# Graph network and transformer kernel: the opening in a new order, the attributes' parts made by GpSimd, and the edge steps spread anew

## The reference

```
xn = layernorm(x)
# graph part
m = concat(xn[src], attr); t = relu(m @ gW1.T + gb1)      # 100000 x 256
h = concat(xn, segment_sum(t, dst)); y = relu(h @ gW2.T); y = y / max(|y|, 1e-12)
# mix part, 4 layers on xn
h = layernorm(x)*g+b;  x += linear_attention(h)  # softmax of k over nodes, of q over features
h = layernorm(x)*g+b;  x += gelu(h @ W1 + b1) @ W2 + b2    # 256 -> 1024 -> 256
# then
x = x + y + mix;  x = x + moe(layernorm(x))      # 16 experts, top 2, layernorm behind it
```

## Time and profile before

| | |
|---|---|
| median of 3 runs | 2307.67 us (2304.2 to 2311.34) |
| the profiled execution | 2316.51 us |
| its span, first to last instruction | 2314.7 us |
| busy: PE, DVE, POOL, ACT | 1936.4, 1443.2, 1357.0, 942.0 us |
| mean granted clock of TensorE | 0.933 |
| keys of layer 0 begin | 175.7 us |
| feed-forward of layer 0 begins | 303.6 us |

### The profile page before, as it was taken

How to read it: one execution, slowest core, us unless ns; L and a number is a source line. 1 busy time by engine, 2 the same in 40 slices (tenths; PEclk the granted TensorE clock), 3 DMA queues, 4 the chain that set the end, 5 groups by cost and what they waited for, 6 DMA issues and landing times.

```text
span 2314.7 us, 31807 instructions
## 1 busy us (share of the span) xinstructions
PE 1936.4 (84%) x10094; PEld 1581.7 (68%) x10094; DVE 1443.2 (62%) x3224; ACT 942.0 (41%) x1964; POOL 1357.0 (59%) x1123
## 2 busy tenths in 40 slices
PE   2437889999888999988899998889999885899990
PEld 1325677778666777866677777668777675788880
DVE  4746686776668677766877777686776557311116
ACT  1215344443545444454444445544444231233330
POOL 4157476667657666775666677567666400566650
PEclk7859999999999999999999999999999976899995
DMA  8564343333533333353333335343333521899997
GB/s 206 177 165 118 90 106 86 83 73 83 150 103 95 88 83 74 81 155 103 90 90 88 74 76 147 104 112 94 83 73 76 113 78 45 270 308 300 306 266 171
DMA packets 275535, 294.05 MB, mean 127 GB/s; under 512 B 146715, under 2 KB 204126, under 8 KB 275390
## 3 DMA queue, kind: packets, MB, share of 16 engines
q0 software_dynamic: 127488, 134.76, 24.5%
q1 hardware_dynamic: 143790, 157.50, 23.0%
q10 hardware_dynamic: 4112, 0.03, 0.1%
HBM read 243.19 MB, written 47.87 MB: 126 GB/s over the span
## 4 chain that ended last, share of the span: by engine, by line
PE 58%; DVE 14%; DMA 12%; ACT 7%; issue 4%; POOL 2%; SPq 2%; DVEq 1%; POOLq 0%; ACTq 0%
PE bank L1262 24%; PE bank L1393 11%; DMA aT<-attr_d 4%; PE bank L1314 4%; PE bank L431 4%; PE bank L432 3%; PE bank L439 3%; DMA TTQ<-zn_d,slot_tok 3%; PE bank L1505 2%; PE bank L1329 2%; PE bank L1513 2%; ACT zr L447 2%; DVE z L479 1%; DMA G<-P_d,src_T 1%; DMA TT<-zn_d,slot_tok 1%
## 5 line engine op out<-in xcount | busy, mean ns | idle before, releaser
L877 POOL DMA_INDIRECT G<-P_d,src_T x896 | 1134.7, 1266 | 627.7 <-DVE z L479 361.9
L447 ACT ACTIVATE zr<-z 125x512 fp32r<-125x512 f32 x448 | 266.7, 629 | 347.9 <-DVE z L479 347.3
L479 DVE TENSOR_TENSOR z<-bank,G 125x512 f32<-125x512 f32 x448 | 289.6, 684 | 150.3 <-PE bank L439 77.4
L453 DVE SCALAR_TENSOR_TENSOR zl<-z,zr 125x512 fp32r<-125x512 f32 x448 | 290.1, 688 | 142.1 <-ACT zr L447 142.0
L1393 PE MATMUL bank<-TT,W_s 128*128 128x250 f32 (+1 forms) x1280 | 361.9, 428 | 15.8 <-ACT hid L1071 15.8
L1262 PE MATMUL bank<-W_s,hid 128*125 128x256 f32 x1600 | 361.1, 379 | 2.2 <-ACT hid L1071 2.2
L1262 PEld LDWEIGHTS bank<-W_s,hid 128*125 128x125 f32 x1600 | 293.9, 187 | 46.0 <-ACT hid L1071 3.8
L1393 PEld LDWEIGHTS bank<-TT,W_s 128*128 128x128 f32 x1280 | 235.7, 190 | 112.5 <-ACT hid L1071 23.0
L431 PE MATMUL bank<-zr,onehot 125*125 125x256 f32 x896 | 273.2, 336 | 20.7 <-DVE zl L453 20.5
L1071 ACT ACTIVATE hid<-bank,b_s 128x375 f32<-128x375 f32 x320 | 163.3, 521 | 270.2 <-PE bank L1393 267.3
L432 PE MATMUL bank<-zl,onehot 125*125 125x256 f32 x896 | 232.1, 289 | 0.0
(11 more groups left out here) (319 smaller groups left out, 2913.9 us busy)
## 6 DMA issues: line engine op xcount, KB each, us to landing
W_s<-in_L_ffn_w SPq DMA_DIRECT2D x64, 512.0 KB, 4.1
hid<-in_L_ffn_w SPq DMA_DIRECT2D x64, 512.0 KB, 4.0
G<-P_d,src_T POOLq DMA_INDIRECT x896, 4.3
TTQ<-nT_d SPq DMA_DIRECT2D x20, 626.0 KB, 6.1
W_s<-in_L_mix_W SPq DMA_DIRECT2D x8, 1024.0 KB, 11.4
nT_d<-TT SPq DMA_DIRECT2D x12, 626.0 KB, 4.9
aT<-attr_d SPq DMA_DIRECT2D x224, 31.2 KB, 2.9
nT_d<-TTQ SPq DMA_DIRECT2D x8, 626.0 KB, 5.3
```

Source lines behind the costliest of these rows:

```text
L447: nc.scalar.activation(zr[:, s, k, :], z[:, k, :], ACT.Relu).then_inc(r_done, 1)
L453: nc.vector.scalar_tensor_tensor(zl[:, k, :], z[:, k, :], 0.0, zr[:, s, k, :].bitcast(f32), ALU.max, ALU.subtract).then_inc(lo_done, 1)
L479: nc.vector.tensor_tensor(z[:, k, :], edge_bank[k][0:ET, :], G[:, ST * s + 2 * k:ST * s + 2 * k + 2, :].rearrange("p j d -> p (j d)"), ALU ...
L877: pool.indirect_dma_start(G[:, j, :], None, P_d[:, :], bass.IndirectOffsetOnAxis(ap=src_T[:, at:at + 1], axis=0)).then_inc(g_in[j], 16)
```

## The change

- X is normalised in place, by groups: statistics of a group, ACT's square root, DVE's product, so that ACT's copy back goes. x is loaded first. P is made in units of two, one and two tiles in the row banks, copied by ACT into `es` and `qe` in turn, written in 30 DMAs instead of 50.
- DVE's opening interleaves: statistics of group g + 1, then a piece of the search for tiles or of the weight parts, then the next group.
- `pool_attr`: POOL splits the attributes, behind the copies of the weight parts and ahead of the scaling of bo and the first gathers. Its buffers are in W1_s and W2_s. A part is written to memory once; `sp_attr` reads it three times, and the constant rows stand in `aT` for good.
- The weights of FF (`weights_B`) come behind the first two attribute loads. xn is written group by group in layer 0's key stage, the zeros of `y_d` in the first FF groups of layers 0 and 1.
- The steps: none before the keys of layer 0, which have 0, 1, 2, 2, 3; FF groups 0 to 2 of every layer have five steps among the eight parts instead of four.

```diff
-        EG_FIRST = 2
-        ST_A, ST_M = 4, 3
-        ST_K = [[3, 2, 2, 2, 3] for l in range(L)]
-        ST_P = [8, 8, 8, 8, 7]
-        ST_B = [EG_FIRST * PG + ST_A + sum(sum(n) + ST_M + sum(ST_P) for n in ST_K[:l]) for l in range(L + 1)]
+        KEY_STEPS = [("", "B", "AB", "AB", "ABD")] + [("ABC", "AB", "AB", "AB", "ABD")] * (L - 1)
+        FF_STEPS = [{0: 0, 2: 1, 3: 2, 5: 3, 6: 4}] * 3 + [{0: 0, 2: 1, 4: 2, 6: 3}] * 2
+        FF_QS = [{1: 1, 2: 2}] * 3 + [{1: 1, 3: 2}] * 2
+        ST_M = 3
+        ST_K = [[len(places) for places in layer] for layer in KEY_STEPS]
+        ST_P = [len(FF_STEPS[g]) + 3 + (g + 1 < NG) for g in range(NG)]
+        ST_B = [sum(sum(n) + ST_M + sum(ST_P) for n in ST_K[:l]) for l in range(L + 1)]
         assert ST_B[L] == NPAIR
...
-            nc.sync.dma_start(aT[:, s, :], attr_flat[ds(e * 128, 128), :]).then_inc(at_in[s], 16)
-        attr_flat = attr_d.rearrange("q i r e -> (q i r) e")
+            nc.sync.dma_start(aT[0:3 * ST * 9, s, :], attr_d[ds(e, 1)].to_broadcast([3, ST * 9, ET])).then_inc(at_in[s], 16)
...
+        def pool_attr(r):
+            def reach(s, n):
+                nc.gpsimd.wait_ge(s, n if isinstance(r, int) else nc.gpsimd.snap(n))
+                if not isinstance(r, int):
+                    nc.gpsimd.sem_inc(settle_pool, 1)
+            ats, ars = parts_of(r)
+            rows = attr_rows.rearrange("p (c e a) -> p c a e", e=ET, a=EA)
+            reach(rows_in, r * (3 * EC * 16) + 3 * EC * 16)
+            for c in range(AC):
+                at, ax, ar = rows[:, c], ats[c % AB], ars[c % 2]
+                if c >= AB:
+                    reach(a_out[c % AB], r * (len(range(c % AB, AC, AB)) * 16) + 16)
+                nc.gpsimd.tensor_copy(ax[:, 0:3, :], at).then_inc(a_split, 1)
+                reach(a_split, r * (4 * AC) + 4 * c + 1)
+                nc.gpsimd.tensor_tensor(ar, at, ax[:, 0:3, :], ALU.subtract).then_inc(a_split, 1)
+                reach(a_split, r * (4 * AC) + 4 * c + 2)
+                nc.gpsimd.tensor_copy(ax[:, 3:6, :], ar).then_inc(a_split, 1)
+                reach(a_split, r * (4 * AC) + 4 * c + 3)
+                nc.gpsimd.tensor_tensor(ax[:, 6:9, :], ar, ax[:, 3:6, :], ALU.subtract).then_inc(a_split, 1)
...
+            load_x(0)
+            sp.dma_start(dst_tiles.rearrange("p (c e) -> p c e", e=SE), dst.rearrange("(c p e) -> p c e", p=EP, e=SE)).then_inc(dst_in, 16)
+            sp.dma_start(gW1, gnn_W1.rearrange("(h p) f -> p h f", p=128)).then_inc(gw_in, 16)
+            sp.dma_start(gW2, gnn_W2.rearrange("(h p) f -> p h f", p=128)).then_inc(gw_in, 16)
+            load_x(1)
+            with nc.allow_non_contiguous_dma(reason="short vectors to columns"):
+                sp.dma_start(w4[:, :, 3:4].squeeze(2), gnn_b1.rearrange("(h p) -> p h", p=128)).then_inc(w4_in, 16)
+            for g in range(2, NG):
+                load_x(g)
...
+            weights_A(0)
+            sp.dma_start(bo8[:, :], bo.rearrange("l d -> (l d)").unsqueeze(0).to_broadcast([128, L * D])).then_inc(bo_in, 16)
+            for g in range(NG):
+                for i, (ta, tb) in enumerate(RP):
+                    sp.wait_ge(row_dve, NRP * g + i + 2)
+                    at = (g * GT + ta) * T
+                    for a, b in SPLIT:
+                        sp.dma_start(P_d[at:at + (tb - ta) * T, :].rearrange("(t p) d -> p t d", p=T)[a:b],
+                                     PROW[g % 2][a:b, ta:tb, :]).then_inc(p_out[g % 2], 16)
+            sp_tables(0)
+            sp.wait_ge(zmade, 2)
+            for e in range(PG):
+                sp_attr(e, e, e, first=True)
+            weights_B(0)
...
+            def keep_xn(g):
+                for a, b in SPLIT:
+                    sp.dma_start(xn_d[g * GT * T:(g + 1) * GT * T, :].rearrange("(t p) d -> p t d", p=T)[a:b],
+                                 X[a:b, g * GT * D:(g + 1) * GT * D].rearrange("p (t d) -> p t d", d=D)).then_inc(xn_out, 16)
+            def clear_y(g):
+                for a, b in SPLIT:
+                    sp.dma_start(y_d[1][g * GT * T:(g + 1) * GT * T, :].rearrange("(t p) d -> p t d", p=T)[a:b],
+                                 zeros[a:b, :].unsqueeze(1).to_broadcast([b - a, GT, D])).then_inc(y_out, 16)
+            sp.wait_ge(hn_done, NT)
...
+            def projected(g):
+                for i, (a, b) in enumerate(RP):
+                    u = NRP * g + i
+                    act.wait_ge(row_full, u + 1)
+                    if i == 0 and g >= 2:
+                        act.wait_ge(p_out[g % 2], g // 2 * NRP * 32)
+                    act.activation(PROW[g % 2][:, a:b, :].rearrange("p j d -> p (j d)"), ROW[(u - ROW_A) % 2][0:T, 0:(b - a) * D],
+                                   ACT.Copy).then_inc(row_dve, 1)
+            input_std(0)
+            act.wait_ge(wT_T, 1)
+            act.activation(W1T[:, :, :].rearrange("p k d -> p (k d)"), bank[6][:, :], ACT.Copy).then_inc(wT_cp, 1)
+            for i in range(2):
+                act.wait_ge(wT_T, 2 + i)
+                act.activation(W2T[:, 2 * i:2 * i + 2, :].rearrange("p k d -> p (k d)"), bank[7 if i == 0 else 5][:, :], ACT.Copy).then_inc(wT_cp, 1)
             for g in range(NG):
-                for j in range(GT):
-                    act.wait_ge(hn_done, g * GT + j + 1)
-                    act.activation(tile(X, g * GT + j), hn[:, j, :], ACT.Copy).then_inc(xcopied, 1)
-                    copy_tile(g * GT + j, j, TT[:, :, j * T:(j + 1) * T], T)
+                for i, (a, b) in enumerate(RP):
+                    u = NRP * g + i
+                    act.wait_ge(ring_full, u + 1)
+                    act.activation(NORM_T[(g + 1) % 2][:, :, a * T:b * T], RING[(u - RING_A) % 3][:, 0:KD * (b - a) * T].rearrange("p (k n) -> p k n", k=KD),
+                                   ACT.Copy).then_inc(ring_act, 1)
+                if g + 1 < NG:
+                    input_std(g + 1)
+                    projected(g)
+            deviations(0, 1, 1)
+            act.wait_ge(par_in, (4 * L + L) * 16)
+            first_norm(0, ring_h1(0, 0), 0)
+            projected(NG - 1)
...
-                        if f - 1 in FF_STEP:
-                            step(e0 + FF_STEP[f - 1])
+                        if f - 1 in FF_STEPS[g]:
+                            step(e0 + FF_STEPS[g][f - 1])
...
+            pe.wait_ge(wT_cp, 3)
+            for g in range(NG):
+                for i, (a, b) in enumerate(RP):
+                    to = ring(NRP * g + i)
+                    for j in range(a, b):
+                        pe.wait_ge(hn_done, g * GT + j + 1)
+                        for k in range(KD):
+                            at = (k * (b - a) + j - a) * T
+                            ins = pe.transpose(to[:, at:at + T], tile(X, g * GT + j)[:, 128 * k:128 * k + 128], ident[0:T, 0:T])
+                    ins.then_inc(ring_full, 1)
+                if g == NG - 1:
+                    normalised_T(0, ring_h1(0, 0), hn)
+                for i in range(NRP):
+                    pe.wait_ge(ring_act, NRP * g + i + 2)
+                    rows_at(NRP * g, i, lambda j: [(NORM_T[(g + 1) % 2][:, k, j * T:(j + 1) * T], W1T[:, k, :]) for k in range(KD)])
+            pe.wait_ge(ws_done, 48)
+            for q in range(4):
+                for h in range(KD):
+                    ins = pe.transpose(bank[3][:, :].bitcast(bf16)[:, q * D + 128 * h:q * D + 128 * h + 128], WS[:, h, q, :], identb[:, :])
+            ins.then_inc(ws_done, 1)
+            pe.wait_ge(wT_cp, 4)
+            pe_tables(0)
+            rounds = round_count(pe)
...
-                        if f in FF_STEP:
-                            step(e0 + FF_STEP[f])
-                        if QIN[g] and f in FF_Q:
-                            queries(g + 1, (FF_Q[f],))
+                        if f in FF_STEPS[g]:
+                            step(e0 + FF_STEPS[g][f])
+                        if QIN[g] and f in FF_QS[g]:
+                            queries(g + 1, (FF_QS[g][f],))
...
+            def input_rows(g):
+                dve.wait_ge(pstd, g + 1)
+                dve.reciprocal(rstd_t[:, g * GT:(g + 1) * GT], stdA[:, g * GT:(g + 1) * GT]).then_inc(prstd, 1)
+                dve.wait_ge(prstd, g + 1)
+                for n in range(g * GT, (g + 1) * GT):
+                    dve.tensor_scalar(tile(X, n), tile(X, n), mvA[:, n:n + 1, 0], rstd_t[:, n:n + 1], ALU.subtract, ALU.mult).then_inc(hn_done, 1)
...
+            input_stats(0)
+            edge_tiles()
+            input_rows(0)
+            input_stats(1)
+            edge_pairs()
+            input_rows(1)
+            input_stats(2)
+            attr_weights()
+            input_rows(2)
+            input_stats(3)
+            first_stats(0)
+            input_rows(3)
+            input_stats(4)
+            bias_rows()
+            input_rows(4)
+            inverse_std(0, 1, 1)
+            normalised(0)
+            dve_tables_b(0)
+            for g in range(1, NG):
+                first_stats(g)
```

(31 more changed lines are left out.)

448 lines of the change are left out of this document (175 added, 273 removed).

## The result

The changed kernel takes 2297.4 us (median of 9 runs, 2292.0 to 2309.4). The kernel before, run beside it, took 2311.4 us: the ratio is 0.9935, with a 95% interval of 0.9917 to 0.9953. It is faster, by 0.65% or some 15 us. I had forecast 2259 and a range up to 2290: the sign was right, the size was not.

The account below looks back on a forecast made before the run. Until 176 us loads, DVE work and DMAs bound it with TensorE idle; TensorE bounds feed-forward groups, POOL second in group 0. Span 2314.7 - 127 + 2 + 76 = 2265.7, in median terms 2259; range 2203 to 2290.

Parts of the forecast that it names:

- POOL's and DVE's work in the opening: Opening: tile numbers at 21.8, POOL's 32 attribute operations 33 us, gathers starting at 78 instead of 93.
- SP comes to P_d behind the small vectors, so I add 3: Opening: SP's issues stand behind the small vectors until about 32, adding 3 us to DVE's 41.9, thus 45.
- Group 1 with one step 14.5: Layer 0's keys: group 0 starts at 62.5 and takes 11.5 us, group 1 takes 14.5, ending at 88.5, made 90.
- +2: Layer 0's keys: xn_d and y_d writes share the queue with attribute loads, costing 2 us.
- 176.5: Forecast start of layer 0's feed-forward, instead of 303.6: a gain of 127 us.
- As many steps as before: Layer 0's keys from group 2 to the feed-forward: 86.5 us, as in layer 1 before.
- +6.6: Feed-forward groups 1 and 2: the ninth step delays the attention by 6.6 us in each of eight groups, 53 together.
- +5.9 by the gathers: Feed-forward group 0: POOL is full, so an extra step costs 6.1 us by gathers, 5.9 through the steps; four groups, 24.
- Rival 1: Feed-forward groups: the ninth step is hidden, costing +17 instead of +76, time 2200; chance 20%.
- Rival 2: Opening: POOL and DVE get in each other's way, 13 to 26 us more, time 2272 to 2285; chance 15%.
- Rival 3: Opening: POOL's 32 operations take 2.6 us or more instead of 1.0, kernel slower, 2323 at 3 us; chance 6%.
- Rival 4: Layer 0's keys: SP's or ACT's queue brings back 40 us, time 2299 to 2310; chance 2%.

Follow-up runs that it names:

- opening_both: Changed kernel with late bias-row work moved behind layer 0's last key group, key group 0's row copy ahead of the weights, short vectors issued between P_d's groups: 2277.0 us.
- sp_last: Changed kernel with key group 0's row copy issued ahead of the weights, bias rows' wait and loads and late loads behind layer 0's last key group: 2285.0 us.
- ninth_late: Changed kernel with feed-forward steps back behind f 0, 2, 4, 6 and the extra one between the queries' transposes and the attention: 2242.2 us.
- softmax_later: Changed kernel with DVE's softmax operations behind step 3 instead of ahead of it in feed-forward groups 1 and 2: 2274.7 us.
- attr_dve: Changed kernel with the attributes split on DVE again, behind its tables, instead of on GpSimd: 2296.2 us.

## Why the prediction was right and wrong

- **POOL's and DVE's work in the opening: right.** Tile numbers at 21.8 (forecast 21.8), first gather 81.9 (78), GpSimd's operations 0.50 to 1.04 us (0.85 to 1.02). The attributes' first edge product comes at 95, not near 84: it follows the product before it on TensorE without a wait, so its place in key group 1 sets it.
- **"SP comes to P_d behind the small vectors, so I add 3": mis-sized.** I took the short vectors into account and gave their delay 3 us. ACT waits 10.7 us at that place, and DVE's first maxima of the keys come at 73.4 where I had 62.5 (TensorE's first product at 70.4). In opening_both, without that wait, they come at 66.0 (63.0).
- **"Group 1 with one step 14.5", so group 2 at 90: the step that failed.** Key group 1 takes 30.8 us, 13.1 of them one wait of ACT, and group 2 starts at 114.9. I followed the moved xn_d and y_d writes through SP's queue and gave them +2, but not what the new order puts ahead of the copy of group 0's rows: weights_B(0), the bias rows and the wait for them to land, which took 2 us ahead of the weights in the kernel before and 14.5 behind them. All of it can be read in the kernel's text, and I named SP's queue only as a rival with 2%. By sp_last it cost 14 us. Together with the short vectors it makes 22 of the 28 us between 176.5 and 204.6 (26 when my +2 for the writes is counted).
- **"As many steps as before", so 86.5 us behind group 2's start: nearly right.** Groups 2 to 4 take 89.8 us in the changed kernel and 89.4 in opening_both. There group 2 starts at 93 where I had 90, since group 0 takes 15.1 instead of 11.5. These are the last 6 us, and no run takes them apart.
- **Groups 1 and 2, "+6.6" each: the mechanism right, the size 1.4 short.** The waits stand where I put them: 1.46, 0.50 and 0.92 for zl, 3.28 for z behind q_softmax. The sums of the fifth step begin 31.0 us into the group (forecast 30.5 to 31.1), and only behind them do the rows leave my working: the attention starts at 38.2 where I had 36.1. Missing was the clock behind the stall, 1.8 of these 2.1. Measured +8.0.
- **Group 0, "+5.9 by the gathers": right**, +6.4, and the runs show it twice: group 0 keeps 63 to 65 us on average wherever the extra step stands, and goes back to 59 when the step is gone.
- **Rival 1, the ninth step hidden (20%):** not in this order, but reachable. ninth_late has it at 1.2 us.
- **Rival 2, GpSimd and DVE in each other's way (15%):** in small, and not by its sign (the first gather comes at 82, not after 95). See the last section.
- **Rival 3, GpSimd's operations at 2.6 us and more (6%):** no, the longest took 1.04.
- **Rival 4, the queue (2%):** its cause is the one that failed my opening, at half its size: 22 us come from the queue and not 40. That its time (2299 to 2310) lies only 2 us off the measured one is luck, since the groups made up the rest. Its chance should have been several times as large, for its place was readable in the kernel's text.
- **Slips that change nothing:** the feed-forward group with PE busy 58.6 of 61 us is group 1 of layer 1, not group 2. In rival 3 the slack of 1.5 us is to be added to the 49 and not taken off, which is what gives the 1.6 us. The bound of 2292 lies just outside the range that ends at 2290.

## What to carry to other kernels

When a change moves work past a queue that issues DMAs in order, write that queue out as a timeline of its own, with every wait in it, before anything is summed: a wait for data to land delays everything that is issued behind it, and the engine that suffers is another one. Moved work pays only where nothing else covers it, so price it again once the other stalls are gone (0 us and 14 us here for the same edit). And place an extra step by what it waits for: in groups 1 and 2 the same ninth step cost 8.0 us between two others and 1.2 us in front of the attention, and about 1 us when it was made in the keys.

## What the runs showed of the hardware

TensorE's clock answered to one stall: behind 3.3 us without a matmul the granted clock was 0.57 for 7 us, and the same instructions took up to twice as long (1.19 for 0.59 us). With the stall gone in softmax_later it stayed at 1.00 in the same group. The stall isn't the only thing that lowers it: groups 1 and 2 of layer 2 in softmax_later, and three such groups in the kernel before, show 0.97 without it.

DVE and GpSimd do hold each other up in the opening. In the changed kernel GpSimd fills agg from 5.61 to 11.03. DVE's timeline beside it:

```profile
8.05 3.27 DVE L1578 COPY mvA<-mv 125x10 f32<-125x10 f32 x1
8.24 3.08 DVE L1600 TENSOR_REDUCE hl<-eT 100x2 f32<-100x1000 int32 x1
9.35 1.97 DVE L1601 TENSOR_REDUCE hl<-eT 100x2 f32<-100x1000 int32 x1
```

All three end at 11.32, just behind the fill. The copy of ten columns takes 0.17 us elsewhere, and the reduction took 1.19 us beside the same fill in the kernel before: the copy is what waits, and the reductions stand behind it. Later an addition of 20x256 takes 0.91 us beside GpSimd's attribute operations (the first runs from 38.06 to 38.74) and 0.41 in attr_dve, where GpSimd does nothing then:

```profile
38.11 0.91 DVE L1626 TENSOR_TENSOR M_s<-M_s,bparts 20x256 f32<-20x256 f32 x1
```

```profile
38.09 0.41 DVE L1625 TENSOR_TENSOR M_s<-M_s,bparts 20x256 f32<-20x256 f32 x1
```

The Trainium skill, SBUF — State Buffer, section "SBUF: two separate sides", says that DVE and GpSimd share a pair of ports as an exclusive lock: a DVE operation in a 2-port mode, or one with two SBUF inputs against a GpSimd operation that reads SBUF, and the GpSimd operation keep each other out for the whole instruction. The traces agree: the copy ends 0.3 us behind the fill, and the addition, with two SBUF inputs, 0.3 us behind GpSimd's first operation. In sum it cost DVE about 3 us at the start and 1.4 in the bias rows, and GpSimd little (0.50 to 1.04 us an operation beside DVE, 0.50 to 1.01 with DVE idle). So it was far from the 13 to 26 us of my second rival.

GpSimd is not far behind DVE in these operations. The same four on 112x375 took 0.68, 1.00, 0.50 and 0.91 us on GpSimd and 0.66, 0.66, 0.36 and 0.55 on DVE.
